# Softplus of the next channel block moved ahead of the state exponentials, with a shorter formula and a split load semaphore

## The reference, cut to what matters

```python
dt = softplus(u @ Wdt + bdt) + 1e-4      # softplus(x) = log1p(exp(-|x|)) + max(x, 0)
b  = u @ Wb + bb
c  = u @ Wc + bc
# for each token s, channel e and state n (16 states):
x[n] = exp(dt * A[n]) * x[n] + dt * b * B_base[n] * u
y    = sum_n c * C_base[n] * x[n] + D * u
x1   = layernorm(u + y)
h    = silu(x1 @ Wg.T) * (x1 @ Wu.T)     # Wg, Wu, Wd = (int - 128) * scale
out  = layernorm(x1 + h @ Wd.T)
```

## Time and profile before

| what | value |
|---|---|
| median of 2 runs | 7790.44 us (7590.4 and 7990.49) |
| profiled execution | 7594.6 us |
| its span, slowest core (core 7) | 7591.8 us |
| the other cores' spans | 7500.6 to 7579.5 us |
| PE busy | 3890.3 us (51%) |
| DVE busy | 2853.6 us (38%) |
| ACT busy | 1658.7 us (22%) |
| recurrence block | from the start to about 4250 us |
| feed-forward block | from about 4250 us to the end |

### The profile page before, as it was taken

The page is one execution under the profiler, slowest core; times in us unless marked ns, Lnnn a source line. Parts: engine busy times, 40 slices in busy tenths (PEclk is TensorE's granted clock), DMA queues, the critical chain, the costliest instruction groups (busy, mean ns, idle before and its releaser), DMA issues.

```text
span 7591.8 us, 50437 instructions; the slowest of 8 cores (7500.6 to 7591.8 us)
## 1 busy us (share of the span) xinstructions
PE 3890.3 (51%) x16672; PEld 1640.2 (22%) x16672; DVE 2853.6 (38%) x4046; ACT 1658.7 (22%) x1981; POOL 387.4 (5%) x428
## 2 busy tenths in 40 slices
PE   1111222221333233323332499949997699949994
PEld 0000111110111011101110244314433243414441
DVE  0322354444688868886888110011100110011101
ACT  2343333333233323332333110000000000000000
POOL 0000000000000000000000011001100111001100
PEclk6555555555666666656666799979998899979997
DMA  8677633334212232222220555946586656945574
GB/s 184 154 162 175 152 87 87 87 87 102 69 40 47 42 71 40 45 44 71 41 43 17 147 155 138 174 101 164 149 159 121 142 152 151 166 106 153 145 139 103
DMA packets 708532, 837.40 MB, mean 110 GB/s; under 512 B 542002, under 2 KB 558770, under 8 KB 691890
## 3 DMA queue, kind: packets, MB, share of 16 engines
q0 software_dynamic: 103040, 487.61, 29.9%
q1 hardware_dynamic: 586802, 321.40, 18.3%
q10 hardware_dynamic: 18432, 25.17, 1.1%
HBM read 885.50 MB, written 159.38 MB: 138 GB/s over the span
## 4 chain that ended last, share of the span: by engine, by line
PE 35%; DVE 26%; DMA 19%; issue 12%; ACT 6%; DVEq 1%; ACTq 0%; SPq 0%; POOL 0%; another core or an unknown queue 0%; POOLq 0%
DVE xp_b L537 19%; PE psD L803 11%; PE psU L786 10%; PE psG L775 10%; DMA ustat<-uwbT 4%; DMA r2r_b<-r2f 4%; PE psP L285 3%; ACT pstg L337 2%; DMA pstg<-gw 2%; DMA pstg<-dw 2%; DMA x1bd<-x1c_b 2%; DMA pstg<-uw 2%; DVE carry L546 1%; DMA dstat<-dwbT 1%; DMA gwbT<-pstg 1%
## 5 line engine op out<-in xcount | busy, mean ns | idle before, releaser
L285 PE MATMUL psP<-u_bf,wstat 128*128 128x512 bf16 (+1 forms) x3840 | 854.0, 387 | 1664.1 <-ACT spA L382 1622.6
L786 PE MATMUL psU<-x1n,ustat 128*128 128x512 bf16 x4096 | 931.3, 381 | 287.9 <-DVE h_t L874 287.9
L405 ACT ACTIVATE ab_b<-dt_b,A_t 128x512 f32<-128x512 f32 (+1 forms) x1024 | 766.6, 772 | 1139.9 <-DVE xp_b L537 1036.1
L775 PE MATMUL psG<-x1n,gstat 128*128 128x512 bf16 x4096 | 942.3, 384 | 125.6 <-DMA ustat<-uwbT 125.3
L537 DVE TENSOR_TENSOR_SCAN xp_b<-ab_b,carry,w_b 128x512 f32<-128x512 f32 x768 | 981.1, 1278 | 47.3 <-ACT ab_b L405 47.3
L803 PE MATMUL psD<-h_t,dstat 128*128 128x512 bf16 x4096 | 901.5, 381 | 38.2 <-DMA dstat<-dwbT 28.9
L285 PEld LDWEIGHTS psP<-u_bf,wstat 128*128 128x128 bf16 x3840 | 392.1, 104 | 2182.0 <-issue 1912.9
L264 PE MATMUL psSm<-r_t,onesc_t 128*1 128x512 f32 x128 | 106.7, 931 | 1447.9 <-ACT spA L412 1447.9
L874 DVE SCALAR_TENSOR_TENSOR h_t<-psU,us_t,sg_b 128x512 bf16<-128x512 f32 x256 | 192.1, 750 | 1645.7 <-PE psU L786 1645.7
L556 DVE SCALAR_TENSOR_TENSOR ya_b<-xp_b,cbb_t,ya_b 128x512 f32<-128x512 f32 x960 | 712.2, 742 | 1.7 <-issue 1.7
L835 ACT ACTIVATE sg_b<-psG,gs_t 128x512 f32<-128x512 f32 x256 | 176.2, 688 | 1910.4 <-PE psG L775 1910.4
(11 more groups left out here) (64 smaller groups left out, 1318.5 us busy)
## 6 DMA issues: line engine op xcount, KB each, us to landing
dstat<-dwbT SPq DMA_DIRECT2D x64, 2048.0 KB, 13.2
gstat<-gwbT POOLq DMA_DIRECT2D x128, 1024.0 KB, 8.9
ustat<-uwbT POOLq DMA_DIRECT2D x128, 1024.0 KB, 11.3
wstat<-wmix POOLq DMA_DIRECT2D x64, 1536.0 KB, 11.9
pstg<-gw POOLq DMA_DIRECT2D x16, 2048.0 KB, 20.8
gwbT<-pstg SPq DMA_DIRECT2D x16, 2048.0 KB, 16.8
pstg<-uw POOLq DMA_DIRECT2D x16, 2048.0 KB, 19.4
uwbT<-pstg SPq DMA_DIRECT2D x16, 2048.0 KB, 10.6
```

Source lines behind the costliest of these rows:

```text
L285: mm = te.matmul(psP[j][:, 0:W_], wstat4[ec % 2][:, j, dc, :], u_bf3[:, dc, off:off + W_], start=(dc == 0), stop=(dc == EC - 1))
L405: se.activation(out=ab_b[n % 4][:, 0:St], in_=dt_b[ec % 2][:, 0:St], func=AF.Exp, scale=A_t[:, ec * N + n:ec * N + n + 1]),
L775: mm = te.matmul(psG[ic % 2][:], gstat4[rot][:, k, ii, :], x1n3[:, k, :], start=(k == 0), stop=(k == EC - 1))
L786: mm = te.matmul(psU[:], ustat4[rot][:, k, ii, :], x1n3[:, k, :], start=(k == 0), stop=(k == EC - 1))
```

## The change

1. The softplus takes two ScalarE instructions per range instead of four: Exp of `psP[0]` with the bias, then Ln of 1 plus that, in place in `spA`. `spB` is gone. `dt_b` is made by a `tensor_scalar` with one input instead of a `scalar_tensor_tensor` with two.
2. The order on ScalarE: step e now does `c_b` of step e, then the softplus of step e+1 (if there is one in the tile), and only then the 16 exponentials of step e. The softplus of a tile's first step stands ahead of `c_b`. All waits are kept, those of softplus e+1 being for projection 0 of step e+1 and for the statistics of step e-1.
3. In the feed-forward block `gstat` and `ustat` get a semaphore each; TensorE waits for both before a pair.

```diff
+                    def sp_blk(t, ec):
+                        rngs = _rngs(TILES[t][2])
+                        ge = t * EC + ec
+                        for ri, (off, W_) in enumerate(rngs):
+                            sm["s_prj"].wait(se, ("prj", t, ec, ri, 0))
+                            if ge >= 2:
+                                pt, pe = divmod(ge - 2, EC)
+                                sm["s_st"].wait(se, ("st", pt, pe))
+                            bcol = bdt_t[:, ec:ec + 1]
+                            v = stag(se.activation(
+                                out=spA[ec % 2][:, off:off + W_],
+                                in_=psP[0][:, 0:W_], func=AF.Exp, bias=bcol))
+                            swait(v)
+                            sm["s_sp"].inc(
+                                se.activation(out=spA[ec % 2][:, off:off + W_],
+                                              in_=spA[ec % 2][:, off:off + W_],
+                                              func=AF.Ln, bias=1.0),
+                                key=("sp", t, ec, ri))
+                    def ce_blk(t, ec):
...
                             for _ in range(6):
                                 prep_sub()
-                            for ri, (off, W_) in enumerate(rngs):
...
+                            if ec == 0:
+                                sp_blk(t, 0)
+                            ce_blk(t, ec)
+                            if ec + 1 < EC:
+                                sp_blk(t, ec + 1)
                             sm["s_vinit"].wait(se, "vinit")
                             sm["s_w"].wait(se, ("w", t, ec, len(rngs) - 1))
...
-                                v = vtag(ve.scalar_tensor_tensor(
+                                v = vtag(ve.tensor_scalar(
                                     out=dt_b[ec % 2][:, off:off + W_],
-                                    in0=spB[ec % 2][:, off:off + W_],
-                                    scalar=eps4_t[:, 1:2],
-                                    in1=spA[ec % 2][:, off:off + W_],
-                                    op0=ALU.add, op1=ALU.add))
+                                    in0=spA[ec % 2][:, off:off + W_],
+                                    scalar1=eps4_t[:, 1:2], scalar2=None,
+                                    op0=ALU.add))
...
-                                    q=16)
-                                sm[f"s_fgs{rot}"].inc(
+                                    key=("fgsg", ts, icg), q=16)
+                                sm[f"s_fus{rot}"].inc(
...
-                                sm[f"s_fgs{rot}"].wait(te, ("fgs", ts, icg))
+                                sm[f"s_fgs{rot}"].wait(te, ("fgsg", ts, icg))
+                                sm[f"s_fus{rot}"].wait(te, ("fgs", ts, icg))
```

More of the change, by code:

```diff
@@ L58 @@
     "s_sq", "s_st", "s_rv", "s_rs", "s_bc", "s_x1", "s_x1b", "s_x1w0", "s_x1w1", "s_x1w2", "s_x1w3", "s_dbg0", "s_dbg1",
-    "s_fx", "s_fgs0", "s_fgs1", "s_fds0", "s_fds1", "s_fg", "s_fu", "s_fsg", "s_fh",
+    "s_fx", "s_fgs0", "s_fgs1", "s_fus0", "s_fus1", "s_fds0", "s_fds1", "s_fg", "s_fu", "s_fsg", "s_fh",
     "s_fdm", "s_fr2", "s_fr2w0", "s_fr2w1", "s_fx1r0", "s_fx1r1",
@@ L144, in build_nc @@
             spA = [msb(f"spA{i}", [128, S0], F32) for i in range(2)]
-            spB = [msb(f"spB{i}", [128, S0], F32) for i in range(2)]
             ab_b = [msb(f"ab_b{i}", [128, S0], F32) for i in range(4)]
@@ L353, in _ @@
                         key="sinit")
+                    def sp_blk(t, ec):
[17 more added lines that the diff above has]
+                    def ce_blk(t, ec):
+                        rngs = _rngs(TILES[t][2])
+                        ge = t * EC + ec
+                        sm["s_prj"].wait(se, ("prj", t, ec, len(rngs) - 1, 2))
+                        if ge >= 2:
+                            pt, pe = divmod(ge - 2, EC)
+                            sm["s_r"].wait(se, ("r", pt, pe))
+                        sm["s_cE"].inc(
+                            se.activation(out=c_b[ec % 2][:],
+                                          in_=psP[2][:, 0:512],
+                                          func=AF.Identity,
+                                          bias=bc_t[:, ec:ec + 1]),
+                            key=("cE", t, ec))
                     for t, (u0, St, wm) in enumerate(TILES):
```

## The result

The changed kernel is slower. Its executions comparable with the profiled one of before took 7799.3 to 7830.9 us against 7579.3 to 7592.5, a ratio of 1.0292 with a 95% interval of 1.0269 to 1.0315. The profiled execution took 7808.0 us, 213 more than the 7594.6 of before; the mean of the eight cores' spans went from 7547 to 7757. The experiments further down ran on three chips, on which the kernel before took 7563 to 7592 us; their ratios are to the time on the same chip.

A forecast was written before the change was run, and what follows sets the result against it. The recurrence was taken to run at VectorE's pace plus its waits, tile 0 adding weight preparation, the second block being TensorE's. Terms 155 + 12 - 12 + 55 + 8.6 - 14.7 = +204 on 7594.6 gave 7799 us, range 7735 to 7890.

The forecast's parts named there:

- how the numbers follow: Closing step: chance 0.73 for the main forecast of 7799 us, range for 8 in 10 of 7735 to 7890.
- -16 and -28: Fast side of the range: bridges half way to the warm bound, -16 us; `wstat` two us earlier in tile 0, -28.
- The 42 bridges: Tiles 1 to 3, steps 1 to 14, `r_t` to next scan: 10.8 us against 7.06, +155 us in all.
- The lower bound of a bridge: Tiles 1 to 3, mid-tile: TensorE's clock warm from the start of projection 0, a bridge +2.95 us longer.
- Tile starts: Tiles 1 to 3, step 0: softplus 1 waits for a cold projection 0, 10.3 us against 6.4, +12 in all.
- Last steps: Step 15 of tiles 1 to 3: no further softplus in the way, 3.1 us instead of 7.06, -12 in all.
- Tile 0: From last chunk to scan: steps 1 to 14 20.9 us, late `wstat`, +55; first step +8.6; last step 1.7, -14.7.
- The split semaphore at zero: Feed-forward block: separate `gstat` and `ustat` waits, one more per pair, 128 in all, priced at zero; otherwise 6 us.
- A (faster): Whole recurrence: the moved softplus's waits are already met, bridges shrink to VectorE's need; 7166 us, chance 0.06.
- B (clock low throughout): Nearly every bridge: TensorE stays at 1.2 GHz through projection 0; +412, 8007 us, chance 0.08.
- C (weights in time): Tile 0: the `wstat` load lands in time, so tile 0 gains 76 us; 7673 us in all, chance 0.1.
- D (no effect, or a gain in the second block): The move does nothing, or the split semaphore gains at most 125 us in the feed-forward block; chance 0.03.

The follow-up runs named there:

- the earlier issue: Changed kernel with GpSimd's queue issuing `wstat` of step e+1 after two of step e's six chunk loads instead of all six; 7639 us, one execution.
- kernel with fillers: Changed kernel plus 130 unread matmuls in each of steps 2 to 15 of tiles 1 to 3, ahead of the statistics; 8216 us, one execution.

## Why the prediction was right or wrong

*The mechanism and the size of the loss were right.* +204 us was forecast; the profiled executions differ by 213, the first blocks by 224 on the mean of the eight cores, and the sum over the bridges is 215. The ratio 7799 / 7594.6 = 1.027 lies at the lower end of the measured interval. It isn't luck: each of the six terms came out near its forecast, as the table shows.

*The step that failed is the last one, how the numbers follow.* The +204 was put on one execution, the profiled 7594.6 us, and the range of 7735 to 7890 was made of the bridges' terms alone. The distance between the two executions shown, 7590.4 and 7990.49, was named and then priced at nothing, without a reason. In its place the runs showed a median of 7960.34 us over ten executions before, 366 above the number that I built on, and of 8080.65 us over eleven of the changed kernel, 191 above the range; six of the eleven took 8080.65 to 8321.4. What makes those six longer stays open here. The range has a slip of its own: the two terms on its fast side, -16 and -28, give 7755 and not 7745.

*What bounds the kernel.* Right: VectorE's scans plus the bridge. In the experiments on formula, place and order the time moved with the bridge: 7.11 us before, 3.04, 5.35, 6.62 and 11.27.

*The 42 bridges.* Expected 10.8, measured 11.21; the difference is in the two terms that depend on the clock. I took 4.1 us for projection 0; with its 0.27 us of drain that makes 4.4, and taking it out of the bridge saved 4.6. The steps in tiles 1 to 3 start near 10 and settle at 11.1 to 11.5, so the mean number of matmuls at the low clock was above the three that I took from the earlier trace rows. In the step shown above, 2590.6 to 2592.6 has a granted clock of 0.50 (1.2 GHz) and 2593 to 2601 one of 1.00 (2.4 GHz), in the windows view of after:

```profile
2590.60:2592.60 2.00, 1.67 (x5) 0.73 (x6) 0.00 (x0) 0.00 (x0) 0.00 (x0) 0.50 0.03 8
2593.00:2601.00 8.00, 8.00 (x39) 3.63 (x37) 3.24 (x6) 4.66 (x8) 0.00 (x0) 1.00 0.00 0
```

The size of this term was off by 0.4 x 42 = 17 us. The lower bound of a bridge, 10.0 us for a clock that is high from the start, was too high: I left the statistics at their time at the low clock, and with the whole bridge at 1.00 it took 8.58.

*Tile starts.* +3.9 each expected, +3.0 measured: projection 0 took 5.8 us there (2018.43 to 2024.24) and not the 6.7 of the burst in the earlier trace rows.

*Last steps.* 3.03 us for 3.1, and 1.5 for 1.7.

*Tile 0.* 20.6 us (core 7) and 20.9 (core 2) for 20.9, with the weights 8.3 us late in the step shown and landing 7.0 (core 7) and 7.3 us (core 2) late on the mean, for 7.4 expected. That the lateness is the cause was settled by the earlier issue.

*The split semaphore at zero.* Right within what one execution tells.

*The rivals.* A (faster) fell, and the kernel with the softplus in the middle shows what its condition was. B (clock low throughout) fell: the bridges never passed 11.50, where it needed 13.6; but the low clock at their start is worth 2.6 of the 4.1 us. C (weights in time) fell, and became true when the load was moved. D (no effect, or a gain in the second block) fell: +224 us in the first block and -13 in the second, of which the split has no part that shows. What would have made the prediction wrong by its own list, the second block moving by more than 20 us, did happen on single cores (core 7: 3411 to 3347 us; core 2: 3359 to 3396) with opposite signs. Core 7's recurrence block grew by 180 us and core 2's by 264, the mean of both being 222; the sum over the bridges of core 7 is 215. So a single core's block length is no test of 20 us here, and the means over the eight cores (+224 and -13 us) are the figures to go by.

## What to carry to other kernels

When an instruction is moved forward on an engine, look at what its inputs are queued behind on the other engines, and count that in front of everything it overtakes: here 1.3 us of ScalarE work brought 8 us of TensorE work onto the path, and it ran there at the low clock behind an idle stretch. The place for work done ahead of time is where its inputs have long been ready and its engine idles between other instructions, not the first place where the program text allows it. And a shared cover hides several late things at once (in tile 0 the load, the single banks, the statistics); taking the cover away shows the next one.

## What the runs showed of the hardware

The granted clock had a level of 0.81 beside 0.50 and 1.00. In the kernel with fillers cores 2, 3, 6 and 7 have it in most of tiles 1 to 3, with fillers, and not in the second block; cores 0, 1, 4 and 5 have it in the second block, without fillers, and not in tiles 1 to 3. So two cores of one die can have it while the other two run at 1.00. Cores 6 and 7 of the kernel before have it too, without any filler, in bursts between 2909 and 3408 us of its span. That the fillers bring it is therefore not shown.

The shortest bridges of that kernel, 8.58 us, are those where fillers at 1.00 ran up to the end of `r_t`. With 4.46 us of idling behind fillers that had run at 1.00, the statistics ran at 0.50, 1.86 us for two matmuls instead of 1.02, and the bridge took 11.49.
